# A recommender tower: tiles in blocks of four partitions, gathers in bursts, pair 2's layer 0 from sums

## The reference

```
e  = stack of tbl_f[ids[:, f]]            # batch 1024, M = 32 fields, D = 16
xk = e
for W in (W0, W1, W2):                    # W: (32, H, 64), H = 32, then 64, 64
    xk = relu(einsum('bmd,bhd,mhk->bkd', e, xk, W))
    z += [sum of xk over d]               # 64 values per batch row
h = relu([z, dense_ctx] @ W_top1 + b_top1)     # 208 -> 512
h = relu(h @ W_top2 + b_top2)                  # 512 -> 256
y = h @ W_top3                                 # 256 -> 1
```

## Time and profile before

| what | value |
|---|---|
| timed runs (median of 3) | 653.85 us |
| profiled execution | 659.91 us |
| its span | 658.1 us |
| TensorE busy | 602.4 us (92%) |
| VectorE busy | 528.1 us (80%) |
| GpSimd busy | 453.6 us (69%) |
| ScalarE busy | 391.4 us (59%) |
| DMA traffic | 103.44 MB, 157 GB/s in the mean |

### The profile page before, as it was taken

The page is one execution under the profiler, slowest core; times in us unless marked ns, Lnnn a source line. Parts: engine busy times, 40 slices in busy tenths (PEclk is TensorE's granted clock), DMA queues, the critical chain, the costliest instruction groups (busy, mean ns, idle before and its releaser), DMA issues.

```text
span 658.1 us, 7277 instructions
## 1 busy us (share of the span) xinstructions
PE 602.4 (92%) x2634; PEld 192.6 (29%) x2634; DVE 528.1 (80%) x281; ACT 391.4 (59%) x631; POOL 453.6 (69%) x306
## 2 busy tenths in 40 slices
PE   1765497789999999999999999999999999999998
PEld 1211122223333333333333333333333333333343
DVE  1065198499989898999999898989898999899700
ACT  0200254386767676767677776858586867677231
POOL 5367365488989788878788878888598855267300
PEclk9997698989999999999999999999999999999999
DMA  4193969594959595968778695949494939450000
GB/s 134 40 226 71 238 168 248 155 236 112 249 129 238 118 249 127 233 148 211 162 204 177 186 198 162 219 146 218 136 222 113 246 92 248 109 97 0 9 8 1
DMA packets 38413, 103.44 MB, mean 157 GB/s; under 512 B 13764, under 2 KB 22856, under 8 KB 30184
## 3 DMA queue, kind: packets, MB, share of 16 engines
q1 hardware_dynamic: 28900, 98.72, 60.8%
q0 software_dynamic: 8192, 2.11, 3.4%
q10 hardware_dynamic: 1284, 2.13, 1.0%
HBM read 97.69 MB, written 4.20 MB: 155 GB/s over the span
## 4 chain that ended last, share of the span: by engine, by line
PE 84%; another core or an unknown queue 5%; issue 4%; ACT 2%; POOL 2%; ACTq 1%; DVE 1%; DMA 1%; SPq 0%; DVEq 0%; POOLq 0%
PE acc L660 65%; PE pair_sum L596 8%; PE pair_sum L576 5%; POOL gath L325 2%; PE pair_sum L640 2%; PE rep L746 2%; PE rep L738 1%; PE rep L739 1%; ACT rep L480 1%; DVE prod L399 1%; ACTq L445 1%; DMA gath<-in_tables,rows_sb 0%; ACT prod_pool L501 0%; SPq L245 0%
## 5 line engine op out<-in xcount | busy, mean ns | idle before, releaser
L399 DVE TENSOR_TENSOR prod<-m_rep,rep 128x2048 f32<-128x2048 f32 x223 | 494.5, 2281 | 56.3 <-DMA m_rep<-x_scratch 28.5
L660 PE MATMUL acc<-prod,w_sb 128*64 128x512 f32 x1792 | 406.0, 602 | 18.3 <-DVE prod L399 13.7
L480 ACT COPY rep<-state 32x512 f32<-32x512 f32 x488 | 283.4, 581 | 59.3 <-DVE prod L399 43.3
L325 POOL DMA_INDIRECT gath<-in_tables,rows_sb x256 | 243.1, 949 | 101.5 <-issue 75.2
L660 PEld LDWEIGHTS acc<-prod,w_sb 128*64 128x64 f32 x1792 | 124.9, 138 | 290.9 <-issue 274.4
L336 POOL TENSOR_TENSOR prod_pool<-m_rep,xb 128x2048 f32<-128x2048 f32 x32 | 146.3, 4571 | 51.7 <-PE acc L660 26.1
L336 POOL TENSOR_TENSOR prod_pool<-x_rot,x_rep 128x2048 f32<-128x2048 f32 x14 | 64.1, 4578 | 9.4 <-DMA x_rot<-x_scratch 9.2
L660 PE MATMUL acc<-prod_pool,w_sb 128*64 128x512 f32 x256 | 60.4, 592 | 0.0
L473 ACT ACTIVATE sums_sq<-pair_sum 128x1024 f32<-128x1024 f32 x30 | 30.8, 1027 | 45.5 <-PE pair_sum L576 25.4
L452 ACT ACTIVATE state<-pair_sum 128x512 f32<-128x512 f32 x16 | 9.6, 597 | 74.2 <-PE pair_sum L640 58.9
L576 PE MATMUL pair_sum<-x0c,sel_sb 32*128 32x512 f32 x120 | 35.7, 672 | 13.8 <-issue 9.5
(11 more groups left out here) (52 smaller groups left out, 102.9 us busy)
## 6 DMA issues: line engine op xcount, KB each, us to landing
m_rep<-x_scratch SPq DMA_DIRECT2D x64, 1024.0 KB
x_rot<-x_scratch SPq DMA_DIRECT2D x30, 512.0 KB
x_rep<-x_scratch SPq DMA_DIRECT2D x15, 512.0 KB
gath<-in_tables,rows_sb POOLq DMA_INDIRECT x256
x_scratch<-gath SPq DMA_DIRECT2D x31, 128.0 KB
x0c<-x_scratch SPq DMA_DIRECT2D x26, 64.0 KB
w_sb<-in_w ACTq DMA_DIRECT2D x2, 512.0 KB
m_rep<-z_sb SPq DMA_DIRECT2D x12, 64.0 KB, 2.3
```

The costliest lines, as they stand in the source:

```text
L325: pool.indirect_dma_start(out=gath[p % 2][:, g, :], out_offset=None, in_=tables, in_offset=bass.IndirectOffsetOnAxis(ap=rows_sb[:, n:n + 1 ...
L399: nc.vector.tensor_tensor(prod[:, number % RING], in0, in1[:, None, :].to_broadcast([128, 2, PAIR]), ALU.mult).then_inc(unit_ready, 1)
L480: last = nc.scalar.copy(rep[v][M * q:M * q + M, CHUNK * a:CHUNK * a + CHUNK], state[l - 1][K * a + M * v:K * a + M * v + M, :])
L660: last = nc.tensor.matmul(acc[K * a:K * a + K, :], w, src[:, k, CHUNK * a:CHUNK * a + CHUNK], start=start and k == 0, stop=stop and k == 1)
```

## The change

- **Tiles.** Partition n of tile t now holds row n // 4 + t: the load's source has 32 rows, each read for 4 partitions (it was 16 rows, 8 partitions). The weights are permuted on the host to match.
- **Gathers.** Four more go out as soon as ScalarE has made its first squares; after pair 0's layer 0 all others up to 68 go in fours, without waiting for VectorE, and after each four GpSimd makes a product of 128 x 256 elements of weights that nobody reads (`unread`).
- **Pair 2's layer 0** uses sums for all four tiles (SUMS_ONLY), like pair 0's: no `x_rep`, `x_rot` loads and no GpSimd product for it, two more pair sums and squares. The first two squares go to `prod_pool`.
- **Pair 1's** direct product moves behind VectorE's unit 4 of slot 1, its pair sums behind slot 0's last unit and slot 1's first, its layer 0 behind units 4 and 5 of slot 1. ScalarE does slot 0's relu first.
- **Replicas.** v = 0 of slots 2 and 3 is now also a `copy_state` by TensorE, behind unit 6 of the slot before.
- **From slot 3 on** the first four gathers of a layer 1 slot stand ahead of its unit, and the pair sums behind units 1 and 4 (2 and 4 in slot 3).

```diff
+BURST = 4
-EARLY = 1
+SUMS_ONLY = (0, 2)
-SUMS_AT = (0, 3)
+def sums_at(i):
+    return (2, 4) if i == POOL_FROM else (1, 4)
-POOL_SEQ = [("x", 2)]
+POOL_SEQ = []
...
-                if p >= EARLY:
-                    if p > EARLY:
-                        x_multiplied(sp, p - 1)
+                if p not in SUMS_ONLY:
+                    if p > 1:
+                        x_multiplied(sp, p - 2 if p - 1 in SUMS_ONLY else p - 1)
...
-                    src = bass.AP(row.tensor, row.offset, [[2 * PAIR, 128 // T], [0, T], [1, 2 * PAIR]])
+                    src = bass.AP(row.tensor, row.offset, [[PAIR, M], [0, Q], [1, 2 * PAIR]])
...
             gather(0, FIRST_RUN)
+            pool.wait_ge(first_sq, 1)
+            gather(FIRST_RUN, BURST)
 
             pool.wait_ge(l0_done, 1)
-            gather(FIRST_RUN, 2 * GPP - FIRST_RUN)
-
-            for n in range(7):
-                pool.wait_ge(unit_ready, 2 * n + 1)
-                gather(2 * GPP + 4 * n, 4)
-            layer0_product(2)
-            for n in range(7, 10):
-                pool.wait_ge(unit_ready, 2 * n + 1)
-                gather(2 * GPP + 4 * n, 4)
-            ahead = 72
+            pool.wait_ge(w1_in, 16)
+            ahead = 4 * GPP + BURST
+            for k, n in enumerate(range(FIRST_RUN + BURST, ahead, BURST)):
+                gather(n, BURST)
+
+                after(pool, burst_out, k)
+                nc.gpsimd.tensor_tensor(unread[:, :, :], w_sb[1][:, 0, 0:T // 2, :], w_sb[1][:, 1, 0:T // 2, :],
+                                        ALU.mult).then_inc(burst_out, 1)
             for i in range(POOL_FROM, NS):
                 l, p = SLOTS[i]
                 if l == 1:
+                    gather(ahead, 4)
                     units(i)
-                    gather(ahead, 4)
...
-                if i == 1:
-
-                    dve.wait_ge(x_in, 16 * (1 + XT))
-                    nc.vector.tensor_tensor(prod_pool[:, 1], x_rot[:, :, :], x_rep[:, None, :].to_broadcast([128, XT, PAIR]),
-                                            ALU.mult).then_inc(second_x, 1)
...
+                    if (i, n) == (1, 4):
+
+                        dve.wait_ge(x_in, 16 * (1 + XT))
+                        nc.vector.tensor_tensor(prod_pool[:, 0], x_rot[:, :, :], x_rep[:, None, :].to_broadcast([128, XT, PAIR]),
+                                                ALU.mult).then_inc(early_x, 1)
...
             relu0(0)
+            relu_slot(0)
             square_x(1)
             square(1, 0)
+            replicate(1, 1)
             square(1, 1)
-            relu_slot(0)
-            replicate(1, 1)
...
-                    square(2, 0)
-                    square(2, 1)
+                    for n in range(ST):
+                        square(2, n)
...
-                    replicate(i + 1, 0)
+                    if i + 1 > COPIED:
+                        replicate(i + 1, 0)
...
-                l = SLOTS[i][0] - 1
-                pe.wait_ge(state_ready[l], 1)
-                if i > 0:
-                    pe.wait_ge(unit_ready, UNIT_BASE[i])
+                l, p = SLOTS[i][0] - 1, SLOTS[i][1]
+                pe.wait_ge(state_ready[l], p + 1)
+                if i == 1:
+                    pe.wait_ge(unit_ready, UNIT_BASE[1])
+                elif i > 1:
+                    pe.wait_ge(unit_ready, UNIT_BASE[i - 1] + v0_units(i - 1))
...
-                    if i == 0 and n in (5, 6):
-                        pair_sums(1, n - 5)
                     if (i, n) == (0, 7):
                         copy_state(1, 0)
+                        pair_sums(1, 0)
+                    if (i, n) == (1, 0):
+                        pair_sums(1, 1)
+                    if (i, n) == (1, 4):
                         layer0_sums(1)
-                        layer0_rest(1)
-                    if (i, n) == (1, 7):
-                        pair_sums(2, 0)
-                    if (i, n) == (2, 1):
-                        pair_sums(2, 1)
-                    if (i, n) == (2, 2):
+                    if i == 2 and n in (0, 1, 2, 4):
+                        pair_sums(2, (0, 1, 2, 4).index(n))
+                    if (i, n) == (2, 5):
                         layer0_sums(2)
-                    if (i, n) == (2, 3):
-                        layer0_rest(2)
+                    if i in (1, 2) and n == 5:
+                        layer0_rest(i)
+                    if i in (1, 2) and n == 6:
+                        copy_state(i + 1, 0)
...
-        return np.asarray(w).reshape(M, 2 * M, K)[(2 * (n // T) + t) % M, M * v + n % M]
+        return np.asarray(w).reshape(M, 2 * M, K)[(n // Q + t) % M, M * v + n % M]
```

More of the change, by code:

```diff
@@ L31 @@
 POOL_TWICE = 29
+COPIED = 3
 FIRST_RUN = 16
+BURST = 4
 WARM_FROM = 10
 WARM = 5
-EARLY = 1
+SUMS_ONLY = (0, 2)
 F1, F2 = 512, 256
@@ L60, with sums_of, rows_to @@
     UNIT_BASE.append(UNIT_BASE[-1] + v0_units(_i) + 4)
+def sums_of(p):
+    return ST if p in SUMS_ONLY else QB
 def sums_to(p):
-    return QB * (p - 1)
-SUMS_AT = (0, 3)
+    return sum(sums_of(_p) for _p in range(1, p))
+def rows_to(p):
+    return p + 1 - sum(_p <= p for _p in SUMS_ONLY)
+def sums_at(i):
+    return (2, 4) if i == POOL_FROM else (1, 4)
 def order(i):
@@ L134, in build @@
         prod_pool = sb("prod_pool", [128, POOL_RING, 2, PAIR])
+        unread = sb("unread", [128, T // 2, K])
         early_sb = xb[0][:, 0:(XT + ST) * 128]
@@ L188, in build @@
         diag_half = sem("diag_half")
-        second_x = sem("second_x")
+        early_x = sem("early_x")
         xsq_ready = sem("xsq_ready")
@@ L202, in build @@
         z_in = [sem(f"z_in{i}") for i in range(2)]
+        burst_out = sem("burst_out")
         top_ready = sem("top_ready")
@@ L221, in x_multiplied @@
             if p == 1:
-                eng.wait_ge(second_x, 1)
+                eng.wait_ge(early_x, 1)
             else:
@@ L332, in product @@
                 if at < POOL_RING:
-                    pool.wait_ge(l0_done, at + 1)
+                    pool.wait_ge(l0_done, at + 2)
                 else:
@@ L339, in layer0_product @@
             def layer0_product(p):
-                pool.wait_ge(x_in, 16 * (1 + XT) * (p - EARLY + 1))
+                pool.wait_ge(x_in, 16 * (1 + XT) * rows_to(p))
                 product(POOL_AT[("x", p)], x_rot[:, :, :], x_rep)
@@ L472, in square @@
                 act.wait_ge(l0_done, p)
-                nc.scalar.activation(sums_sq[:, n, :], pair_sum[:, :], SQUARE).then_inc(sq_ready, 1)
+                t = n if p in SUMS_ONLY else XT + n
+                dst = prod_pool[:, p - 1, t, :] if t < XT else sums_sq[:, t - XT, :]
+                nc.scalar.activation(dst, pair_sum[:, :], SQUARE).then_inc(sq_ready, 1)
             def replicate(i, v, chunks=2):
@@ L574, in pair_sums @@
                     pe.wait_ge(sq_ready, sums_to(p) + n)
+                t = n if p in SUMS_ONLY else XT + n
+                sel_of = sel0_sb[:, t, :] if t < XT else sel_sb[:, t - XT, :]
                 for a in range(2):
-                    last = nc.tensor.matmul(pair_sum[:, CHUNK * a:CHUNK * a + CHUNK], sel_sb[M * a:M * a + M, n, :],
+                    last = nc.tensor.matmul(pair_sum[:, CHUNK * a:CHUNK * a + CHUNK], sel_of[M * a:M * a + M, :],
                                             x0c[p % 2][M * a:M * a + M, :], start=True, stop=True)
@@ L627, in layer0_sums @@
                 pe.wait_ge(sq_ready, sums_to(p + 1))
+                if p in SUMS_ONLY:
+                    for t in range(XT):
+                        layer0_tile(half_sb[:, t, :], prod_pool[:, p - 1, t, :], t == 0, False)
                 for t in range(QB):
-                    layer0_tile(w0_sb[:, XT + t, :], sums_sq[:, t, :], t == 0, False)
+                    layer0_tile(w0_sb[:, XT + t, :], sums_sq[:, t, :], p not in SUMS_ONLY and t == 0, False)
             def layer0_rest(p):
[L632 to L637, removed]
+                if p not in SUMS_ONLY:
+                    x_multiplied(pe, p)
+                    at = 0 if p == 1 else POOL_AT[("x", p)] % POOL_RING
+                    for t in range(XT):
+                        last = layer0_tile(w0_sb[:, t, :], prod_pool[:, at, t, :], False, False)
+                    if p > 1:
+                        last.then_inc(pool_used, 1)
+                diag = wdiag0_sb if p in SUMS_ONLY else wdiag_sb
                 pe.wait_ge(xsq_ready, p + 1)
                 for a in range(2):
-                    last = nc.tensor.matmul(acc0[K * a:K * a + K, :], wdiag_sb[M * a:M * a + M, :],
+                    last = nc.tensor.matmul(acc0[K * a:K * a + K, :], diag[M * a:M * a + M, :],
                                             xsq[M * a:M * a + M, :], start=False, stop=True)
@@ L706, in _ @@
                         pool_unit(0)
-                    if i >= 3 and l == 1 and p + 1 < NP and n in SUMS_AT:
-                        pair_sums(p + 1, SUMS_AT.index(n))
-                    if i == 0 and n in (5, 6):
-                        pair_sums(1, n - 5)
```

(21 more changed lines are left out.)

## The result

The changed kernel takes 635.77 us (median of four runs, 635.66 to 635.88) and the kernel before 653.62 on the same chip: a ratio of 0.973 (95% interval 0.9713 to 0.9748), 17.9 us less. Its profiled execution took 635.88 us, with a span of 633.9. The prediction said 631.0, between 619 and 650, so direction and range held, and the value was 4.8 us too low.

What follows compares the result with a forecast made beforehand. TensorE was taken to bound the steady steps, so only slot 3's earlier start (106.5 instead of 131.87, 25.4 us) gains: profiled 659.91 becomes 634.5, and the middle of median cases 628.5 and 634.5 gives 631 us, 8-in-10 range 619 to 650.

Steps and rivals of the forecast that it cites:

- What bounds the kernel: From slot 3 on TensorE bounds, 34.47 us per step; all gain comes from starting slot 3 earlier, 25.4 us.
- Rival 2: Slots 0 to 2: small products don't part the gather runs, TensorE's signals stay late, 649 us; chance 0.12.
- Slot by slot: Worked times of slots 0 to 2, from slot 0's end at 54.4 to slot 3's start at 106.5 us.
- The step that failed by 1.2 us: Slot 2: pair 2's two more pair sums, 2 x 1.1 us on TensorE, fit in time VectorE's units leave free.
- Unit 6 of slot 2 done meanwhile: End of slot 2: layer 0 at 102.7, relu 103.3, unit 6 done by then, copy ready at 105.4 us.
- The median's offset: Whole run: profiled execution 6.06 us over median; 628.5 if everywhere, 634.5 if late signals worsen under the profiler; middle 631.
- Rival 1: Tile loads stay at 230 GB/s; slot 0 costs 3.2 us more, median 633 to 639, say 636; chance 0.20.
- Rival 3: Layer 2 slot's end: joined run of nine gathers holds product buffers, 4 us per pair, 683 us; chance 0.07.
- runs of four that a product of 4.6 us separates: Gathers of the kernel before: after such runs the profile shows no long piece that no engine explains.
- Rival 4: Pair 1's x product waits on its late rows: 2 to 4 us, inside the range; no separate chance given.
- the prediction's working of this rule: At the x product, GpSimd and VectorE exclude one another on SBUF: one small product, 0.7 us, added once.

Runs made afterwards that it cites:

- e3: The changed kernel without the small unread products, so its early gathers follow each other unbroken: 705.16 us, 1.053 of the kernel before.
- e3b: The changed kernel without the small unread products, run again in the third group on another chip: 692.88 us, 1.0475 of before.
- e4: The kernel before with only a small product behind each four gathers up to slot 3, old tile layout: 655.43 us, 0.985 of before.
- e2b: The changed kernel with the old tile layout (blocks of eight partitions), run again in the third group: 660.77 us, 0.9977 of before.
- e7: The changed kernel with ScalarE's eight copies in place of TensorE's copy for v = 0 of slots 2 and 3: 660.27 us, 0.9953 of before.
- e5: The kernel before with new tile layout and small products behind each four gathers up to slot 3: 644.60 us, 0.9852 of before.
- e1: The kernel before with only the new tile layout (blocks of four partitions): 673.35 us, 1.004 of before (0.995 to 1.013).
- e2: The changed kernel with the old tile layout (blocks of eight partitions), first run: 665.57 us, 0.998 of before.
- e6: The changed kernel with the four gathers of a layer 1 slot back behind its unit (runs of 5, 4 and 7): 635.70 us, 0.971 of before.
- v1: The changed kernel with pair 2's sums behind units 0 to 3 of slot 2, layer 0 behind unit 4, replica directly after: 652.29 us, 0.9826 of before.
- e8: The changed kernel with pair 2's rows loaded and its direct product by VectorE behind unit 4 of slot 2: 638.81 us, 0.9766 of before.
- c1: The changed kernel once more, unaltered, as yardstick of its group on the even chip: 635.61 us, 0.9708 of before.

## Why the prediction was right, and where it was off

**What bounds the kernel** held: the steady step stayed at 34.47 us and the gain is the earlier start of slot 3. Removal showed what had only been read from the rows: long gather runs hold the signals (e3, e3b), and parting them alone brings 1.5% (e4). Rival 2 did not come on the even chips. Its 649 us are 0.993 of before, and e2b and e7 of the third group, with their small products and late signals, lie at 0.998 and 0.995. So that it stayed away from the result was in part the luck of the chip.

**Slot by slot**, the working against the trace: slot 0 ends at 54.90 (54.4), x loads go out at 59.73 (59.2 to 59.5), slot 1 starts at 58.22 (57.8), the x product stands at 69.21 without a wait and ends at 71.50 (69.7, 72.0), slot 2 starts at 81.39 (81.5) and ends at 100.26 (100.3). A small product took 0.75 us (0.7), and tile loads ran at 352 and 396 GB/s where 342 was taken.

**The step that failed by 1.2 us** is slot 2's: the two more pair sums lie "in time that VectorE's 2.2 us per unit leaves free". Four of its units have a pair sum behind them, which makes 1.87 + 1.06 = 2.93 us of TensorE per unit against VectorE's 2.2 (83.83 and 85.77, and 92.67 to 97.31, of the chain). TensorE falls behind, is the bound from 83.83 on, and ends layer 0 at 103.62 instead of 102.7. "Unit 6 of slot 2 done meanwhile" holds for the relu alone (103.67), as the replica waits behind the unit until 105.49; but this costs little against the forecast, which had 2.7 us from layer 0's end to the replica where the trace has 2.9. Slot 3 began at 107.69 instead of 106.5: 24.2 us gained instead of 25.4.

**The median's offset** is the mis-sized term that matters. Of the two cases that were named (628.5, 634.5) I took the middle, 631. The changed kernel's profiled execution is 0.1 us above its median (635.88 and 635.77), e5's level with it (644.59 and 644.60), and before's was 6.1 above. So the difference is not everywhere, which was the condition for 628.5; 634.5 plus the 1.2 us above gives 635.7. By the medians 22.9 us were forecast and 17.9 came. Why before's profiled execution was the long one stays open. The recorded reason, late signals being worse under the profiler, is not borne out: e3b holds its signals longest, and its profiled execution is 2.3 us under its median (690.55 and 692.88); and a single profiled execution of before is on record. The two cases were 7.3 and 1.3 us off; the middle, 4.8 off, had no row behind it.

**Rival 1** (tile loads stay at 230 GB/s) is refuted by the windows. What the faster loads are worth in us is not: alone nothing (e1), and in the changed kernel e2 and e2b mix it with the late signals. By the start of slot 1 it is 3.1 us (61.34 in e2b, 58.22).

**Rival 3** (the joined run of nine) is refuted on the even chip by e6. The prediction's "runs of four that a product of 4.6 us separates" is short of what the steady stage of before has: runs of five and seven as well, as rival 3 itself says of seven.

**Rival 4:** the x product did not wait for its rows. In the changed kernel no small product lay beside it, but a gather did; in e2 and e2b a small product did, as told below.

## What to carry to other kernels

When a chain of waits shows an unknown queue, compare the end of the instruction that signals with the start of the one that waits, and look at what every engine was issuing in between: here a product of 0.75 us that nobody reads, behind every fourth gather, was worth 1.5%, and without it the whole change would have been a loss of 5%. Don't take the profiled execution's excess over the median for a constant: it was 6.1 us for the kernel before and 0.1 for the one after. And before work is put into an engine's slack, add it to that engine's own time per unit, 2.93 us here against the 2.2 of the engine it was to hide behind.

## What the runs showed of the hardware that I had not expected

- TensorE's signals came late in long runs of gathers: by 4.9 us in the run of 12 and 12.0 us in the run of 32, by 52 us in the run of 52 of e3b. Early in such a run they did not: VectorE's units of slot 0 go on without a wait up to 52.44 in e3b, 15 gathers into its run. Where they came through lies near the run's end: in the run of 32 0.6 us before its last gather ends (74.14), in the run of 12 1.5 us after (123.84), in e3b 8.8 us after. In those last us of e3b no engine works and no DMA engine moves anything (window; busy us of each engine, granted clock, DMA share, GB/s), so neither a gather nor its transfer is under way:

```profile
100.60:108.20 7.60, 0.00 (x0) 0.00 (x0) 0.00 (x0) 0.00 (x0) 0.00 (x0) 0.50 0.00 0
```

  What holds the signals is not shown, only that they come late (to ScalarE, and in before to VectorE) and that small products between the gathers end the long holds.
- The same kernel form behaves otherwise from chip to chip. On the even chip no signal was late with bursts of four; on the other two squares and relus were late in e2, e2b, e4, e7 and v1 too, by up to 7.0 us each (that is e7's square at 110.26, behind matmuls that end at 103.26). What differs between the chips was not found.
- GpSimd can be held by VectorE. Beside the x product, which reads two tiles of SBUF (69.21 to 71.50), GpSimd's gather took 2.24 us instead of 0.94:

```profile
70.07 2.24 POOL L339 DMA_INDIRECT gath<-in_tables,rows_sb  x1 [0.30 <-issue]
```

  It ends 0.8 us after the product. Eight other runs show the same, with 2.1 to 2.95 us; in before and in e2b a gather that began within 0.02 us of the product kept its 0.94. A small product is held too, in e2 beside the x product from 73.89 to 76.17 for 2.87 us instead of 0.74, in e2b for 1.96:

```profile
73.90 2.87 POOL L377 TENSOR_TENSOR unread<-w_sb 128x256 f32<-128x256 f32 x1
```

  VectorE's units, whose replica is in PSUM, lengthened none. The Trainium skill ("SBUF — State Buffer", SBUF: two separate sides) has a VectorE operation with two SBUF inputs and a GpSimd operation that reads SBUF exclude each other; the traces agree, at a price of 1.3 us once for the gather (which reads its row numbers from SBUF) and 2.1 for the small product, where the prediction's working of this rule had 0.7.
- Tile loads whose source rows repeat for four partitions instead of eight, with the same piece length, ran at 352 to 396 GB/s in the changed kernel (359 in e7) against 218 and 230.
- TensorE's granted clock had fallen in the stage of late signals of before (0.50 from 59 to 62 us, 0.54 from 70 to 80), and the four L576 matmuls at 59.50 took 2.07 us; after, the four of L596 took 1.13 at 58.10, with the clock at 1.00 from 50 to 60 (0.83 from 60 to 70, where L687's eight took 3.63). While nothing ran on TensorE in e3b (60 to 105 us) it was 0.50, which is 1.2 GHz. A stall can be paid once more in the first matmuls behind it, as e8's 3.61 us show. It need not be: c1 has the same wait of 1.33 us ahead of the same eight matmuls, and they took 1.94 us, with the clock at 1.00 from 60 to 70.
